# Edge filter of a vision tower on 64-row tiles of TensorE, its halo from greyscale rows, norms on ScalarE

## The reference

```
gray  = einsum('bchw,c->bhw', x, (0.2989, 0.587, 0.114))
edges = conv 3x3 of gray with scharr and its transpose, 'SAME'
h     = (|edges_0| + |edges_1|) / 2                      # 8 x 256 x 256
h     = h + attention(layernorm(h))   # q, k, v: 256x256; q, k times Wp per head; 16 heads of 16
h     = h + ffn(layernorm(h))         # own norm, 256 -> 1024 silu -> 256, dequantised weights
```

## Time and profile before

| | us |
|---|---|
| median of 3 runs | 309.68 |
| lowest, highest | 309.09, 311.72 |
| profiled execution, its own time | 308.78 |
| its span in the profile | 307.0 |
| TensorE busy in the span | 286.5 (93%) |
| VectorE busy | 213.6 (70%) |
| ScalarE busy | 161.4 (53%) |
| GpSimd busy | 132.1 (43%) |

### The profile page before, as it was taken

One profiled execution on the slowest core, in us unless ns is written; L12 is line 12 of the kernel. 1 busy time (PEld: TensorE's weight loads), 2 busy tenths in 40 slices (PEclk: granted clock), 3 DMA queues, 4 the chain that ended last, 5 costly groups with the idle time before them and its releaser, 6 DMA issues.

```text
span 307.0 us, 6170 instructions
## 1 busy us (share of the span) xinstructions
PE 286.5 (93%) x2280; PEld 224.3 (73%) x2280; DVE 213.6 (70%) x423; ACT 161.4 (53%) x304; POOL 132.1 (43%) x250
## 2 busy tenths in 40 slices
PE   0499999999999999999999999898999999999996
PEld 0378878887677766666666666565898988989976
DVE  8978984785799988888889888634835734642332
ACT  1391453523333478768777876776344434434440
POOL 7605240330200018862859562066759489500000
DMA  6978019895398971678582000000000200200202
GB/s 211 324 191 270 2 69 288 181 217 206 108 281 252 326 270 55 183 185 270 162 174 76 4 3 2 0 2 2 0 1 2 69 2 0 68 2 0 70 0 68
DMA packets 26631, 35.30 MB, mean 115 GB/s; under 512 B 5082, under 2 KB 15594, under 8 KB 26602
## 3 DMA queue, kind: packets, MB, share of 16 engines
q1 hardware_dynamic: 26440, 34.77, 38.0%
q10 hardware_dynamic: 162, 0.15, 0.1%
HBM read 24.42 MB, written 10.49 MB: 114 GB/s over the span
## 4 chain that ended last, share of the span: by engine, by line
PE 81%; DVE 13%; ACT 3%; issue 2%; ACTq 0%; DVEq 0%
PE bank L1139 46%; PE bank L1257 9%; PE bank L1209 8%; PE bank L1232 4%; PE bank L1237 4%; DVE negmax L848 3%; PE bank L1275 3%; PE bank L1267 1%; DVE gray L725 1%; PE bank L1161 1%; PE bank L1283 1%; PE bank L1176 1%; DVE qk_l L838 1%; DVE gray L724 1%; DVE xn L813 1%
## 5 line engine op out<-in xcount | busy, mean ns | idle before, releaser
L848 DVE TENSOR_REDUCE negmax<-bank 128x2 f32<-128x512 f32 x128 | 82.0, 684 | 6.1 <-PE bank L1209 5.8
L1047 ACT ACTIVATE probs<-bank 128x512 f32<-128x512 f32 x128 | 66.1, 602 | 28.2 <-PE bank L1237 28.2
L902 DVE TENSOR_TENSOR y_l<-yf,y_h 128x512 fp32r<-128x512 f32 x32 | 23.7, 743 | 39.1 <-ACT yf L1073 39.0
L1070 ACT ACTIVATE y_h<-bank,b1col 128x512 fp32r<-128x512 f32 x32 | 22.1, 689 | 47.8 <-PE bank L1139 47.8
L1139 PE MATMUL bank<-w_h,y_h 128*128 128x256 f32 x128 | 36.9, 289 | 2.5 <-DVE y_l L902 2.1
L1139 PE MATMUL bank<-w_h,y_l 128*128 128x256 f32 x128 | 36.2, 282 | 0.0
L1139 PE MATMUL bank<-w_l,y_h 128*128 128x256 f32 x128 | 36.2, 282 | 0.0
L1257 PE MATMUL bank<-probs,vals 128*32 128x256 f32 x512 | 34.3, 385 | 0.0
L1209 PE MATMUL bank<-ks,qs 48*128 48x256 f32 x256 | 32.2, 329 | 1.3 <-DVE negmax L848 0.7
L1209 PEld LDWEIGHTS bank<-ks,qs 48*128 48x128 f32 x256 | 19.3, 184 | 15.7 <-DVE negmax L848 6.4
L1139 PEld LDWEIGHTS bank<-w_h,y_h 128*128 128x128 f32 x128 | 24.4, 190 | 4.6 <-DVE y_l L902 3.6
(11 more groups left out here) (147 smaller groups left out, 612.6 us busy)
## 6 DMA issues: line engine op xcount, KB each, us to landing
xr<-in_x SPq DMA_DIRECT2D x8, 768.0 KB, 9.0
qs<-qk_parts SPq DMA_DIRECT2D x48, 128.0 KB, 3.3
ks<-qk_parts SPq DMA_DIRECT2D x48, 128.0 KB, 3.4
qk_parts<-qk_h SPq DMA_DIRECT2D x16, 256.0 KB, 3.2
qk_parts<-qk_l SPq DMA_DIRECT2D x16, 256.0 KB, 3.5
wraw<-in_L_ffn_fc_q SPq DMA_DIRECT2D x4, 512.0 KB, 4.6
wscale<-in_L_ffn_fc_scales SPq DMA_DIRECT2D x4, 512.0 KB, 6.7
out<-osb SPq DMA_DIRECT2D x16, 128.0 KB, 1.8
```

The costliest lines, as they stand in the source:

```text
L848: eng.tensor_reduce(negmax[:, b % 2, u, v], entry_bank(key)[:, :].rearrange("p (t k) -> p t k", t=NT), AX.X, ALU.max, negate=True).then_in ...
L902: eng.tensor_tensor(y_l[:, p % 2, f], yf[:, n % 2], y_h[:, p % 2, f].bitcast(fp32), ALU.subtract).then_inc(s_y, 1)
L1047: eng.activation(probs[:, n % PBUF], p2[n % 4][:, :], ACT.Exp).then_inc(s_exp, 1)
L1070: eng.activation(y_h[:, p % 2, f], src, ACT.Silu, bias=b1col[:, f:f + 1])
```

## The change

The edge filter works on row tiles of 64 image rows: `tok(p, t)` multiplies partitions 0 to 63 into one bank and 64 to 127 into the next, with both filter kernels side by side in the 128 output columns; each half gets a halo matmul of 27 partitions. ScalarE reads each bank in two activations of 64 partitions. The halo operand is built from whole pixel rows: ScalarE loads them first of all, POOL makes greyscale and its two parts, and nine transfers (three by ScalarE, six by SyncE ahead of the load of image 3) stack them shifted. The weights of the halo are made by VectorE from small masks (`halo_bands`). `xn` is written by ScalarE as rstd * h + shift, POOL makes the shift. gray_high of images 2 and 3 moves to POOL, the copies of the transposed weights move to VectorE. TensorE does the edge products of pair 0 before the weights' transposes, and the edges of pair 1 are complete before the transposes of pair 0. VectorE does the weights after the moments of pair 0, then the value weights, and the edges and moments of pair 1 before `xt_low` of pair 0. The diff, cut to its core (what is left out: the smaller buffers and semaphores, the masks, which VectorE now turns into 18 half-wide band pieces instead of VectorE and POOL into nine each, and removed functions):

```diff
-                    turns.extend(("xt", p, kf) for kf in range(KE))
-                    turns.extend(("tok", p + 1, i) for i in (2, 3))
+                    steps = [[("xt", p, kf) for kf in range(KE)], [("tok", p + 1, i) for i in (2, 3)]]
+
+                    for step in steps if p else steps[::-1]:
+                        turns.extend(step)
...
+        def stack_halo(eng, dx):
+            lo, hi = max(0, 1 - dx), E - max(0, dx - 1)
+            for part, src in enumerate((halo_h, halo_h, halo_l)):
+                first = 9 * part + dx
+                eng.dma_start(halo[first:first + 7:3, :, :, lo:hi].rearrange("r t b w -> r (t b) w").bitcast(fp32),
+                              src[:, lo + dx - 1:hi + dx - 1].bitcast(fp32)).then_inc(s_halo, 16)
...
             load_x(2)
+            eng.wait_ge(s_border, 7)
+            eng.wait_ge(s_halo_g, 1)
+            for dx in (1, 2):
+                stack_halo(eng, dx)
             load_x(3)
...
+            eng.wait_ge(s_halo_x, 16 * 6)
+            eng.tensor_scalar(halo_g[:], halo_x[:, 0], GRAY[0], 0.0, ALU.mult, ALU.add)
+            for c in (1, 2):
+                ins = eng.tensor_scalar(halo_x[:, c], halo_x[:, c], GRAY[c], 0.0, ALU.mult, ALU.add)
+            link(ins)
+            for c in (1, 2):
+                link(eng.tensor_tensor(halo_g[:], halo_g[:], halo_x[:, c], ALU.add))
+            link(eng.tensor_scalar(halo_h[:], halo_g[:], 1.0, 0.0, ALU.mult, ALU.add))
+            eng.tensor_tensor(halo_l[:], halo_g[:], halo_h[:].bitcast(fp32), ALU.subtract).then_inc(s_halo_g, 1)
...
+            def gray_high(b):
+                eng.wait_ge(s_gray, b + 1)
+                eng.tensor_scalar(gray_h[:, (b // 2) % 2, :, b % 2, 1:E + 1], gray[:, b % 2], 1.0, 0.0, ALU.mult, ALU.add).then_inc(s_grayh, 1)
...
             def tok_rstd(p, t):
                 js = slice(2 * t, 2 * t + 2)
                 eng.wait_ge(s_mv, NT * p + t + 1)
+                eng.tensor_scalar(nmean_a[:, js], mv[:, js, 0], -1.0, 0.0, ALU.mult, ALU.add)
                 link(eng.tensor_scalar(vareps[:, js], mv[:, js, 1], EPS, 1.0, ALU.add, ALU.mult))
-                eng.tensor_tensor(rstd[:, js], vareps[:, js], mhalf[:, js], ALU.pow).then_inc(s_rstd, 1)
+                link(eng.tensor_tensor(rstd[:, js], vareps[:, js], mhalf[:, js], ALU.pow))
+                eng.tensor_tensor(shift_a[:, js], nmean_a[:, js], rstd[:, js], ALU.mult).then_inc(s_rstd, 1)
...
-            gray_low(2)
-            gray_low(3)
+            for b in (2, 3):
+                gray_high(b)
+                gray_low(b)
...
+                for k in range(2):
+                    for dx in range(3):
+                        w = s_all[:, 9 * k + 3 * dy + dx:9 * k + 3 * dy + dx + 1]
+                        if dy == 0:
+                            ins = eng.tensor_scalar(band[:, dx, k], masks[:, dy], w, None, ALU.mult)
+                        else:
+                            ins = eng.scalar_tensor_tensor(out=band[:, dx, k], in0=masks[:, dy], scalar=w,
+                                                           in1=band[:, dx, k], op0=ALU.mult, op1=ALU.add)
...
+                for half, col in enumerate((HALF - 1, 0)):
+                    for k in range(2):
+                        for t in range(NT):
+                            dst = halo_b[:, t, half, HALF * k + col:HALF * k + col + 1]
+                            eng.tensor_copy(dst, halo_ws[:, k, half:half + 1])
+                for t in range(NT):
+                    for k in range(2):
+                        col = HALF * k + (HALF - 1) * (1 - t)
+                        ins = eng.tensor_copy(halo_b[:, t, 1 - t, col:col + 1], halo_ws[:, k, 2 + t:3 + t])
+                ins.then_inc(s_halo_b, 1)
...
-            eng.wait_ge(s_bandp, 1)
-            for i in range(2):
-                link(eng.tensor_tensor(band1[:], band1[:], bandp[:, i], ALU.add))
-            link(eng.tensor_copy(band_h[:, 1], band1[:]))
-            eng.tensor_tensor(band_l[:, 1], band1[:], band_h[:, 1].bitcast(fp32), ALU.subtract).then_inc(s_band1, 1)
-            halo_low(slice(0, 2), 1)
+            halo_bands()
             gray_add(2)
+            for op in range(2):
+                eng.wait_ge(s_wt, op + 1)
+                eng.tensor_copy(wtr[:, op], bank[op][:, :]).then_inc(s_wtc, 1)
             gray_add(3)
-            halo_low(slice(2, B), 2)
...
-            eng.wait_ge(s_wld, 16 * (NT + 1))
-            link(eng.tensor_copy(wqk_h[:, :, 2 * E:], wv_src[:]))
-            eng.tensor_tensor(wqk_l[:, :, 2 * E:], wv_src[:], wqk_h[:, :, 2 * E:].bitcast(fp32), ALU.subtract).then_inc(s_wready, 1)
+
+            eng.wait_ge(s_ident, 1)
+            link(eng.tensor_reduce(picked[:], ident[:].rearrange("p (v c r u) -> p u v c r", v=2, c=8, r=2)[:, :, :, 0], AX.XY, ALU.add))
+            eng.tensor_copy(pick[:], picked[:]).then_inc(s_pick, 1)
 
...
-            tok_normalise(0, 0)
-            tok_normalise(0, 1)
             for op in range(2):
                 weights(op)
+            eng.wait_ge(s_wld, 16 * (NT + 1))
+            link(eng.tensor_copy(wqk_h[:, :, 2 * E:], wv_src[:]))
+            eng.tensor_tensor(wqk_l[:, :, 2 * E:], wv_src[:], wqk_h[:, :, 2 * E:].bitcast(fp32), ALU.subtract).then_inc(s_wready, 1)
             for p in range(PAIRS):
                 more = p + 1 < PAIRS
                 if more:
                     edges(p + 1, 0)
                 if more:
+                    if p == 0:
+                        tok_moments(1, 0)
+                        edges(1, 1)
+                        tok_moments(1, 1)
                     for kf in range(KE):
                         xt_low(p, kf)
                     for i in range(2):
                         if ("tok", p + 1, i) in HEAD_AT:
                             largest(HEAD_AT["tok", p + 1, i])
-                    tok_moments(p + 1, 0)
+                    if p:
+                        tok_moments(p + 1, 0)
                     if p + 2 < PAIRS:
                         gray_add(2 * p + 4)
-                    edges(p + 1, 1)
-                    tok_moments(p + 1, 1)
+                    if p:
+                        edges(p + 1, 1)
+                        tok_moments(p + 1, 1)
                     for i in (2, 3):
                         if ("tok", p + 1, i) in HEAD_AT:
                             largest(HEAD_AT["tok", p + 1, i])
-                    tok_normalise(p + 1, 0)
...
-                    if i == 0 and more:
-                        tok_normalise(p + 1, 1)
...
+            for t in range(NT):
+                for r, row in enumerate((t * P + HALF - 1, t * P + HALF, P - t)):
+                    first = B * (NT * r + t)
+                    eng.dma_start(halo_x[first:first + B], x[:, :, row, :]).then_inc(s_halo_x, 16)
...
+            def edge(p, t):
+
+                for half in range(2):
+                    key = ("tok", p, 2 * t + half)
+                    rows = slice(HALF * half, HALF * (half + 1))
+                    wait_filled(eng, key)
+                    eng.activation(hid[rows, p, t].rearrange("p b e -> p (b e)"), turn_bank(key)[0:HALF, :], ACT.Abs)
+                    if p >= 1 and half == 0:
                         eng.wait_ge(s_edges, NT * (p - 1) + t + 1)
-                    dst = absd[:, t]
-                else:
-                    dst = hid[:, p, t].rearrange("p b e -> p (b e)")
-                eng.activation(dst, turn_bank(key)[:, :], ACT.Abs).then_inc(freed(key), 1)
+                    eng.activation(absd[rows, t], turn_bank(key)[HALF:P, :], ACT.Abs).then_inc(freed(key), 1)
+
+            def tok_normalise(p, t):
+                eng.wait_ge(s_rstd, NT * p + t + 1)
+                if p >= 1 and t == 0:
+                    wait_filled(eng, ("xt", p - 1, KE - 1))
+                for j in (2 * t, 2 * t + 1):
+                    ins = eng.activation(xn[:, j // 2, j % 2, :], hid[:, p, j // 2, j % 2, :], ACT.Identity, scale=rstd[:, j:j + 1],
+                                         bias=shift_a[:, j:j + 1])
+                ins.then_inc(s_xn, 1)
...
             gray_scale(0)
+            gray_high(0)
             gray_scale(1)
-            gray_high(0)
             gray_high(1)
-            eng.wait_ge(s_halo, 16 * 3 * NT)
-            halo_high(slice(0, 2))
-            for op in range(2):
-                eng.wait_ge(s_wt, op + 1)
-                eng.activation(wtr[:, op], bank[op][:, :], ACT.Copy).then_inc(s_wtc, 1)
+            eng.wait_ge(s_border, 7)
+            eng.wait_ge(s_halo_g, 1)
+            stack_halo(eng, 0)
             gray_scale(2)
             gray_scale(3)
-            halo_high(slice(2, B))
-
-            eng.wait_ge(s_band1, 1)
-            edge(0, 0)
-            gray_high(2)
-            gray_high(3)
-            for i in range(1, 4):
-                edge(0, i)
+            for t in range(NT):
+                edge(0, t)
+            tok_normalise(0, 0)
+            edge(1, 0)
+            tok_normalise(0, 1)
+            edge(1, 1)
```

(67 more changed lines are left out.)

174 lines of the change are left out of this document (63 added, 111 removed).

## The result

The changed kernel took **317.73 us** (median of 4 runs, 317.05 to 322.81) against 309.4 before beside it: ratio 1.026, 95% interval 1.021 to 1.032. (The ratio leaves out the execution of 322.81 us, which fell in a slower state of the chip.) The forecast was 309.3 us, with a range to 312.5; the result lies outside it, on the slower side. The profiled execution took 318.39 us with a span of 316.6, against a span of 307.0 before.

What follows compares the result with a forecast made beforehand. TensorE was taken to set the pace, with VectorE as late at the handover. Five us saved in later pairs, less 2.8 at the start and 2.6 at half pace, moved the handover 0.4 us earlier: 309.3 us, range 304.5 to 312.5.

Steps and rivals of the forecast that it cites:

- the start up to the first QKV: Everything before pair 0's first QKV matmul: work is queued, not saved; start at 41.3 us against 38.48, 2.8 us later.
- (b): At the start, POOL turns the halo rows into greyscale parts in 3.9 us, to 15.4 us.
- (d): At the start, image 3 lands 4.9 us after its issue, nothing else being in flight, at 24.2 us.
- (a): At the start, halo-row loads, issued first on ScalarE's queue, land at 11.5 us, between bounds 8.7 and 14.8.
- (c): At the start, SyncE issues six stacking transfers ahead of image 3, taking 3.88 us, to 19.3 us.
- Rival 3: At the start, image 3 comes still later behind POOL's split of the halo rows: 312.6 us; chance 0.13.
- rival 4: In the edge tiles, paired matmuls do not run side by side, so tiles cost 4.66 us again: 317.3 us; chance 0.04.
- Half pace: After a 6 us gap before pair 0's QKV, TensorE runs at half its clock, losing 2.6 us.
- Rival 1: TensorE keeps its pace over the gap before pair 0's QKV: 306.7 us; chance 0.22.
- The later pairs: Each later first-stage pair takes 16.8 us against 19.15, with cheaper row tiles less a TensorE stall.
- the stall ahead of the second row tile: In later pairs, TensorE waits 1.2 us for ScalarE to read the first tile's edges from PSUM.
- Behind the handover: From the attention stage on, nothing is edited, so the change costs or gains only what the handover moves.

Runs made afterwards that it cites:

- both gates open: Changed kernel with image 3 loaded ahead of SyncE's wait and pair 0's halo matmuls reading zeros, so neither waits: 309.4 us, ratio 1.0035.
- the stack alone: Changed kernel with image 3 first, halo matmuls behind the fold, and SyncE's later loads held until the stack has landed: 313.36 us, ratio 1.016.
- the last two runs: Kernel before with row tiles and ScalarE norms in pairs 2 and 3, later pair 3 transposes: 306.12 us; the same plus six filler matmuls: 305.15 us.
- the run before them: Kernel before with row tiles and ScalarE norms in pairs 2 and 3, POOL's band copies behind its first reciprocal roots: 307.23 us, ratio 0.993.
- the last run: Kernel before with row tiles and ScalarE norms in pairs 2 and 3, later pair 3 transposes and six filler matmuls: 305.15 us, ratio 0.990.

## Why the prediction was wrong

**The step that failed is the start up to the first QKV, steps (b) to (d) and what I put behind them.** The prediction had 41.3 us, the trace 48.98. Its terms:

- (a) Halo rows at 11.5: measured 11.94. Right, with some luck: it was taken as the middle of 8.7 and 14.8 (which is 11.75), not from a row.
- (b) POOL's split 3.9 us: measured 5.1. The tensor_scalar took 0.54, 0.81 and 0.81 us where I had 0.41 from the earlier trace rows, and every linked step adds 0.07 us between them.
- (c) Six stacking issues 3.9 us: measured 5.5, 0.7 to 1.1 each. Rival 3 had named this possibility with 2 us.
- (d) Image 3 lands 4.9 us behind its issue "because nothing else is in flight": measured 7.7. The stack was in flight, and so were the loads issued behind. How much of the 2.8 us each of them took was not tried.

That puts image 3 at 30.33 instead of 24.2. Of the rest, 18.65 us instead of 17.1 went from there to the first QKV. That these are near each other is luck, for the path was another. Eight edge activations take 4.9 us (0.61 each) where the earlier trace rows had given 0.54, the value weights 1.1 us of VectorE instead of 2.90 (40.41 to 41.5), and VectorE did not run without a gap, as I had it. The chain that ended last goes through the stack, TensorE at half pace and ScalarE's queue instead, where the norms of pair 0 stand ahead of the edges of pair 1.

**What the prediction left out altogether is the wait of TensorE for the stack.** It followed the stacking only as something in front of image 3 on SyncE, never to its own reader. The runs show it to be worth as much as the image: opening one gate moves the first QKV by 1.1 us or not at all, opening both by 8.1 us. A sum along one path would have been wrong even with every term right, since it would have called image 3 first a cure.

**Rival 3** had the right sign and the right place (image 3 behind the split, each us of it a us of handover), with the wrong condition: it was to decide from a landing of the halo rows near 15. They came at 11.94 and the time was still lost behind them. That rival 4's 317.3 us is near the measured time is chance; what it says is refuted below.

**Half pace:** 2.6 us predicted, 1.1 measured in pair 0's QKV (matmuls 0.43 us apart until 52.1). The granted clock is 0.50 there, as the Trainium skill's TensorE: Matmul & The Clock Gate, Part 1 has it after idleness; the level was right, the length was not. I had it fall once; it fell first in the wait for the stack, and the fold took 5.2 us (30.49 to 35.7) instead of the 2.8 of the run with filler matmuls, where it had full pace. Rival 1 (no fall) is refuted by the same rows.

**The later pairs:** the stall ahead of the second row tile was predicted at 1.2 us and measured at 1.34 and 0.9; the edge matmuls of a row tile at 2.56 + 0.2 us, measured 2.95 (59.05 to 62.00, with both halos). The period came out at 17.42, against 16.8 predicted; the last stretch at 33.8, against 31.9. VectorE starts it 5.4 us behind the edges instead of 4.9 and is idle 1.36 us ahead of the second ones (1.77 in the earlier trace rows), where I had counted on 0.4. Rival 4 (pairs not side by side) is refuted by 0.23 us for two.

**Behind the handover** I said that nothing is edited and nothing moves. TensorE waits 1.2 us for negsplit at 129 us. In the chain of waits this goes back through POOL, which works on the first FFN weights ahead of negsplit, to their scales, issued by SyncE at 116.5 and landed 7.3 us later; before, they were issued at 106.9. That this wait belongs to the later loading was read from the chain and not tried by itself. The wait is also 1.2 us with both gates open, 0.6 us with the stack alone, and below 0.5 in the kernel without the halo path, so lateness by itself does not explain it; it stays open.

In sums of the trace, the first QKV is 10.5 us late and half pace behind it takes 1.1; 1.7 come back in the period and 1.5 in the last stretch, which leaves 8.4 at the handover, and 1.2 behind it make the 9.6 of the spans.

What the norms do by themselves was not tried. That they, with the row tiles, bring the period from 18.87 to 17.41 us rests on the profiled executions of the last two runs, which also have the later transposes and POOL's copies moved; in the run before them the clock fell in that period, which took 18.98.

## What to carry to other kernels

When work is turned into transfers, follow each of them to its own reader as well as to what is queued behind it, and look for a second gate of the same lateness before believing in a cure for the first. A transfer that writes to few partitions has few DMA engines behind it: price it by its bytes at that share, not by the landing of an image. A wait costs twice if TensorE comes out of it at half pace. Time taken from the fullest engine is worth what the next engine leaves: here the row tiles gained 0.3 us in a period while VectorE had the norms and 1.7 without them, and the start, which was made late to get them for pair 0, cost more than all later pairs could return.

## What was not expected of the hardware

- Nine transfers of 48 KB to three partitions each ran at 48 to 78 GB/s in total, with 0.1 to 0.2 of the DMA engines busy, while wide loads reached 365 GB/s on the same core.
- ScalarE took 0.59 us for 64 partitions of 512 columns, as much as for 128 (0.60 for an edge activation of pair 0 in the kernels with row tiles in the later pairs), and 0.61 us from one to the next.
- The clock fell to its lower level in a busy stretch, behind waits of 0.9 to 1.35 us, in some executions and not in others of the same kernel. In the last run one execution, in which it fell, took 307.7 us and the five others 305.0 to 305.3. What decides between them stays open.
